# An expert's rows in parts: two halves of the down product in two banks, a write for each tile of rows

## What is computed

```python
w_topk, e_topk = jax.lax.top_k(probs, TOP_K)                 # 2 of 8 experts
buf = jnp.zeros((E, CAPACITY, H)).at[e_flat, pos].set(x_rep, mode='drop')
h = _rms(buf, norm_w[:, None, :])
gate = jax.nn.gelu(jnp.einsum('ech,ehf->ecf', h, Wg), approximate=False)
up = jnp.einsum('ech,ehf->ecf', h, Wu)
buf_out = jnp.einsum('ecf,efh->ech', gate * up, Wd) + buf
exp_out = buf_out[e_flat, jnp.minimum(pos, CAPACITY - 1)]
combined = x + (w_topk.reshape(-1)[:, None] * exp_out * keep).reshape(N, TOP_K, H).sum(axis=1)
```

## Time and profile before

| | |
|---|---|
| median of 3 runs | 454.93 us (454.25 to 458.86) |
| the profiled execution, own time | 458.62 us |
| its span, first to last instruction | 456.9 us |
| mean granted clock of TensorE, 1.00 being 2.4 GHz | 0.934 |
| busy share of the span: PE, DVE, POOL, ACT | 85%, 68%, 59%, 49% |
| chain that ended last, by engine | PE 60%, DVE 14%, issue 7%, POOL 6%, DMA 5% |

### The profile page before, as it was taken

How to read it: one execution, slowest core, us unless ns; L and a number is a source line. 1 busy time by engine, 2 the same in 40 slices (tenths; PEclk the granted TensorE clock), 3 DMA queues, 4 the chain that set the end, 5 groups by cost and what they waited for, 6 DMA issues and landing times.

```text
span 456.9 us, 7235 instructions
## 1 busy us (share of the span) xinstructions
PE 390.0 (85%) x2470; PEld 180.1 (39%) x2470; DVE 309.9 (68%) x722; ACT 223.6 (49%) x498; POOL 268.3 (59%) x242
## 2 busy tenths in 40 slices
PE   8985869999999999999899889998777697998810
PEld 2432524444334344444345334432324343654510
DVE  4786877757876867777966998864376456665514
ACT  1550433867776667667586655666630121322200
POOL 7383183678559688478586569688504350355650
PEclk9998998999999999999999999998985588999985
DMA  8594766005505009705005000008100011221118
GB/s 240 88 293 118 117 135 96 16 0 105 143 1 108 2 5 248 230 22 87 2 13 95 3 0 9 15 18 279 58 0 30 26 49 52 70 83 60 44 47 275
DMA packets 30461, 37.48 MB, mean 82 GB/s; under 512 B 4757, under 2 KB 25045, under 8 KB 30101
## 3 DMA queue, kind: packets, MB, share of 16 engines
q1 hardware_dynamic: 24378, 29.91, 27.6%
q0 software_dynamic: 2240, 4.21, 3.0%
q10 hardware_dynamic: 3808, 2.92, 2.3%
HBM read 28.56 MB, written 12.75 MB: 90 GB/s over the span
## 4 chain that ended last, share of the span: by engine, by line
PE 60%; DVE 14%; issue 7%; POOL 6%; DMA 5%; ACT 3%; SPq 2%; another core or an unknown queue 2%; POOLq 0%; DVEq 0%; ACTq 0%
PE ps_av L1128 14%; PE ps_st L1099 12%; PE ps_slot L1020 12%; DVE neg_max L1346 5%; PE ps_slot L1024 5%; POOL parts L800 3%; PE ps_st L964 3%; PE ps_slot L1159 2%; PE ps_st L1203 2%; DMA k_parts<-part_all 2%; ACT probs L910 1%; POOL probs L732 1%; PE ps_st L1107 1%; PE ps_slot L1213 1%
## 5 line engine op out<-in xcount | busy, mean ns | idle before, releaser
L910 ACT ACTIVATE probs<-ps_st 128x512 f32<-128x512 f32 (+3 forms) x384 | 168.5, 494 | 106.5 <-PE ps_st L1099 99.9
L1346 DVE TENSOR_REDUCE neg_max<-ps_slot 128x1 f32<-128x640 f32 (+7 forms) x184 | 175.8, 989 | 56.8 <-PE ps_slot L1024 54.7
L732 POOL TENSOR_TENSOR probs<-probs,f_all 128x960 f32<-128x960 f32 (+2 forms) x65 | 123.7, 1904 | 10.3 <-ACT probs L910 5.5
L1020 PE MATMUL ps_slot<-k_stack,q_stack 128*128 128x512 bf16 (+3 forms) x384 | 101.0, 333 | 10.5 <-DVE neg_max L1346 5.6
L1099 PE MATMUL ps_st<-q_stack,k_stack 128*128 128x512 bf16 (+3 forms) x384 | 104.0, 331 | 4.8 <-ACT probs L910 3.6
L1128 PE MATMUL ps_av<-probs,v_all 128*9 128x512 f32 (+3 forms) x768 | 81.1, 496 | 2.3 <-POOL probs L732 1.6
L729 POOL TENSOR_SCALAR_AFFINE_SELECT probs<-probs 128x512 f32<-128x512 f32 x58 | 37.1, 639 | 68.4 <-ACT probs L910 68.2
L1024 PE MATMUL ps_slot<-b_all,flip_b 128*128 128x240 bf16 (+2 forms) x288 | 66.5, 256 | 0.0
L1099 PEld LDWEIGHTS ps_st<-q_stack,k_stack 128*128 128x128 bf16 x384 | 34.6, 98 | 76.9 <-ACT probs L910 54.8
L1020 PEld LDWEIGHTS ps_slot<-k_stack,q_stack 128*128 128x128 bf16 x384 | 36.0, 99 | 44.5 <-DVE neg_max L1346 12.3
L800 POOL DMA_INDIRECT parts<-probs,e_tok x32 | 31.1, 972 | 38.1 <-DVE probs L1661 27.4
(11 more groups left out here) (188 smaller groups left out, 408.0 us busy)
## 6 DMA issues: line engine op xcount, KB each, us to landing
q_stack<-q_parts SPq DMA_DIRECT2D x21, 192.0 KB
slots<-in_c_rows_dram SPq DMA_DIRECT2D x4, 528.0 KB, 9.9
probs<-slots SPq DMA_DIRECT2D x8, 264.0 KB
parts<-in_c_rows_dram SPq DMA_DIRECT2D x4, 512.0 KB, 9.6
q_stack<-parts SPq DMA_DIRECT2D x4, 512.0 KB, 5.5
k_stack<-k_parts SPq DMA_DIRECT2D x14, 128.0 KB
f_all<-g_vec ACTq DMA_DIRECT2D x1, 1536.0 KB, 12.6
q_parts<-part_all SPq DMA_DIRECT2D x16, 96.0 KB, 3.5
```

The lines of the kernel that those rows point to most:

```text
L732: pool.tensor_tensor(pr, pr, f_of[:, n % (H // HG), :, fo:fo + hi - lo], ALU.mult).then_inc(near_done, 1)
L910: act.activation(probs[:, u % PBUF, g, c0:512], ps_st[:, ST_NO[what] % 3, c0:512], ACT.Exp, scale=SCALE).then_inc(exp_done, 1)
L1020: pe.matmul(ps_slot[:, slot, o + lo:o + hi], q_stack[:, buf, t // MT, g, t % MT * P:(t % MT + 1) * P], k_stack[:, buf, lo // CW, g, 0:hi - ...
L1346: dve.tensor_reduce(neg_max[:, t // MT, heads[0]:heads[-1] + 1, t % MT], src, AX.X, ALU.max, negate=True).then_inc(slot_used, 1)
```

## The change

The down product is split: the tiles of rows 0 and 1 go to `ps_slot[:, 0, ...]`, the bank that the transposes of the same buffer use, tiles 2 and 3 to `ps_slot[:, 1, ...]` as before. Each half raises `eo_ps`. Each scale waits for its own half. Each write waits for its own scale. The row numbers are made in `weights_of_rows`, in arrays with a place for every expert, and raise semaphores of their own (`row_done`, `tok_done`). Since transposes now share a bank with rows 0 and 1, `turn` waits until two tiles of the expert before in that buffer are scaled.

```diff
-        e_row_tok = sb("e_row_tok", [P, 2, 4])
-        e_tok = sb("e_tok", [P, 2, 4], U32)
+        e_row_tok = sb("e_row_tok", [P, E_NUM, 4])
+        e_tok = sb("e_tok", [P, E_NUM, 4], U32)
...
             def scatter_rows(e, i):
-                pool.wait_ge(eo_done, 6 * (e + 1))
+                pool.wait_ge(tok_done, e + 1)
                 for j in range(4):
+                    pool.wait_ge(eo_done, 4 * e + j + 1)
...
                 if positive(e - 1):
                     pe.wait_ge(eT_sb, e - 1)
+                    pe.wait_ge(eo_done, 4 * (e - 2) + 2)
...
-                        mm = pe.matmul(ps_slot[:, 1, i * 512 + j * C:i * 512 + (j + 1) * C],
+                        mm = pe.matmul(ps_slot[:, j // 2, i * 512 + j * C:i * 512 + (j + 1) * C],
...
-                mm.then_inc(eo_ps, 1)
+                    if j % 2:
+                        mm.then_inc(eo_ps, 1)
...
                 dve.tensor_tensor(e_wt[:, i, 2, :], e_wt[:, i, 0, :], e_wt[:, i, 1, :], ALU.mult).then_inc(ewt_done, 1)
+                dve.tensor_tensor(e_row_tok[:, e, :], e_row_tok[:, e, :], e_wt[:, i, 0, :], ALU.subtract).then_inc(row_done, 1)
                 dve.wait_ge(ewt_done, 2 * e + 1)
                 dve.tensor_tensor(e_wt[:, i, 2, :], e_wt[:, i, 2, :], a2, ALU.add).then_inc(ewt_done, 1)
+                dve.wait_ge(row_done, e + 1)
+                dve.tensor_copy(e_tok[:, e, :], e_row_tok[:, e, :]).then_inc(tok_done, 1)
...
             def scale_rows(e, i, n):
-                dve.wait_ge(eo_ps, e + 1)
                 if positive(n):
                     dve.wait_ge(scattered[i], 64 * n)
-                dve.tensor_tensor(e_row_tok[:, i, :], e_row_tok[:, i, :], e_wt[:, i, 0, :], ALU.subtract).then_inc(eo_done, 1)
-                dve.wait_ge(eo_done, 6 * e + 1)
-                dve.tensor_copy(e_tok[:, i, :], e_row_tok[:, i, :]).then_inc(eo_done, 1)
                 for j in range(4):
-                    dve.tensor_scalar(e_out[i][:, j, :], ps_slot[:, 1, i * 512 + j * C:i * 512 + (j + 1) * C], e_wt[:, i, 2, j:j + 1], None,
+                    dve.wait_ge(eo_ps, 2 * e + j // 2 + 1)
+                    dve.tensor_scalar(e_out[i][:, j, :], ps_slot[:, j // 2, i * 512 + j * C:i * 512 + (j + 1) * C], e_wt[:, i, 2, j:j + 1], None,
                                       ALU.mult).then_inc(eo_done, 1)
```

More of the change, by code:

```diff
@@ L472, in layer_kernel @@
         eo_done = sem("eo_done")
+        row_done = sem("row_done")
+        tok_done = sem("tok_done")
         scattered = [sem(f"scattered{i}") for i in range(2)]
@@ L797, in scatter_rows @@
             def scatter_rows(e, i):
-                pool.wait_ge(eo_done, 6 * (e + 1))
+                pool.wait_ge(tok_done, e + 1)
                 for j in range(4):
-                    pool.indirect_dma_start(parts[:, :], bass.IndirectOffsetOnAxis(ap=e_tok[:, i, j:j + 1], axis=0),
+                    pool.wait_ge(eo_done, 4 * e + j + 1)
+                    pool.indirect_dma_start(parts[:, :], bass.IndirectOffsetOnAxis(ap=e_tok[:, e, j:j + 1], axis=0),
                                             e_out[i][:, j, :], None, bounds_check=2 * (B * T + 2 * CAP) - 1,
@@ L1632, in weights_of_rows @@
                 if positive(e - 1):
-                    dve.wait_ge(eo_done, 6 * (e - 1))
+                    dve.wait_ge(eo_done, 4 * (e - 1))
                 a1, a2 = slot_in[i][:, :, C], slot_in[i][:, :, C + 1]
-                dve.tensor_scalar(e_row_tok[:, i, :], slot_in[i][:, :, C + 3], 2.0, 1.0, ALU.mult,
+                dve.tensor_scalar(e_row_tok[:, e, :], slot_in[i][:, :, C + 3], 2.0, 1.0, ALU.mult,
                                   ALU.add).then_inc(ewt, 1)
```

## The result

The changed kernel takes 454.23 us (median of 20 runs, 450.75 to 460.97) against 456.76 us for the kernel before on the same chip (median of 20 runs, 453.03 to 460.84): **a ratio of 0.9936, with a 95% interval of 0.9917 to 0.9955**. That is 2.0 to 3.8 us faster; the ratio leaves out slow runs, the medians do not. The forecast was 2.0 us slower. The measured time lies in the forecast's range, and the change is under the 1% that was given a chance of 0.70, but it went the other way.

What follows compares the result with a forecast made beforehand. It took TensorE to bound the expert stage up to about 420 us and GpSimd's row writes from 421. Waits of +3.6 and early writes of -1.6 gave +2.0 us on the median 454.93: 456.9 us, range 453.0 to 460.5.

Steps and rivals of the forecast that it cites:

- Regimes and GpSimd's price: Expert stage: TensorE's pace to about 420 us, 5.7 us an expert; GpSimd's row writes from 421 us, 5.1 an expert.
- Early writes, 1.6 us: GpSimd's writes for experts 6 and 7 start after the first scale, so the end comes 1.6 us earlier.
- The waits of single writes: Three writes an expert get their own wait on GpSimd: taken as nothing, upper bound 2.9 us at the end.
- Row numbers ahead and restart: Row numbers moved before VectorE's gating: 0.10 us an expert; TensorE restarting after each new wait: 0.15 us.
- The new wait, 3.6 us: TensorE's transposes wait for two scaled tiles: 2.44 us over experts 0 to 4, 3.6 later with restarts and row numbers.
- The two disturbances: Late scales of experts 2 and 4, releaser unnamed: TensorE idle 0.94 and 2.04 us, lower clock behind them about 1.7.
- three signs of being wrong: Transposes start without waiting, end writes over 1.3 us apart, or granted clock below 1.00 between 395 and 415 us.
- Rival 3: Both disturbances in the expert stage go, saving 4.7 us: 448.6 to 452.2 us, chance 0.08.
- rival 1: TensorE's new waits add up, the forecast itself: 455.7 to 459.5 us, centre 456.9, chance 0.55.
- Rivals 2 and 4: Waits hidden, only the gain left: 453.3 us, chance 0.17; disturbances become serial: 459.2 with one, 461.5 with two, chance 0.12.
- The clock (rival 5): TensorE's clock falls in the new waits, 1.7 us a fall: 458.6 with one, 460.3 with two, chance 0.08.
- The rule on the shared port: VectorE in two-port mode would hold GpSimd's writes up to 0.34 us, 2.7 at the end; the sum held nothing.

Runs made afterwards that it cites:

- late_writes: Changed kernel, but GpSimd waits for all four scales of an expert before writing its first tile: 457.18 us, ratio 0.9984.
- half_writes: Kernel before, but GpSimd writes only rows 0 and 1 of each expert, leaving out half the routed rows: 446.01 us, ratio 0.9813.
- landed: Kernel before, but GpSimd begins an expert's writes only when those of the expert ahead have landed: 457.36 us for one run (kernel before beside it 454.44).
- other_bank: Changed kernel, but rows 0 and 1 of the down product go where the other buffer's transposes were, so the wait is met at once: 453.81 us, ratio 0.9945.

## Why the prediction was wrong, step by step

- **Regimes and GpSimd's price.** The price was right: 969 to 992 ns a write, 1.28 apart at the end. The second regime was not the stage's own: GpSimd's hold on the chain from 421 us on began with the second disturbance, and without it GpSimd holds only the last four writes.
- **Early writes, 1.6 us.** Right: the last write stands 1.52 us nearer to expert 7's down product, and the first write of expert 1 starts 1.18 us after its first scale (1.1 forecast). Taken back by *late_writes*, the ratio goes from 0.9936 to 0.9984, about 2.2 us, with intervals that touch and late counts that came back with it, so this is no clean price; the trace shows 0.54 us in the way to the end. The waits of single writes cost nothing: 0.30 before expert 7's first write, the usual pause.
- **Row numbers ahead and restart.** The row numbers, 0.10 an expert, cost nothing that the rows show: from the first instruction of `weights_of_rows` to the gating it is 1.66 us with them (406.17 to 407.83) and was 1.67 at expert 4 without them (413.15 to 414.82). The restart was put at 0.15; a step grew by 0.95 us with 0.77 of idle time in it, which leaves 0.18.
- **The new wait, 3.6 us.** Right in kind, too small in size: 5.2 us. The forecast took the lateness from single experts of before (0.22 to 0.81) and had 4.4 for six experts at full clock; it left expert 5 out for a low clock that was the second disturbance's. In the settled rhythm each gating starts 1.38 us behind the down product (406.45 to 407.83 above), as late as at expert 4 before, where expert 1 had 1.15; that makes 0.77 each time. The difference comes for the most part from one instruction. The second half of the fold starts 0.50 us into a row write (406.82 and 407.32 above) and takes 0.59 us, in all five such experts, and as much in the changed kernel with the loads ahead, where no slot load runs; in *half_writes*, where no write stands beside it, it takes 0.33 to 0.35. At expert 1 and at expert 4 before:

```profile
396.10 0.33 DVE L1623 TENSOR_SCALAR probs<-k_stack,e_norm 128x256 f32<-128x256 f32 x1
...
414.31 0.59 DVE L1623 TENSOR_SCALAR probs<-k_stack,e_norm 128x256 f32<-128x256 f32 x1
```

- **The two disturbances: the step that failed.** The sum was made on an execution that had them, and held them to be the same after the change: "the terms come from the stage's own steps, not from the disturbances". They are a result of how GpSimd's writes follow one another, and the change alters that: they cost 5.2 us before, and after it no idle time of that kind is left. A term of -5.2 us that the sum held at 0 is what turned its sign. The forecast even had the pieces: it priced GpSimd's writes, and eight of them follow one another from 407.42 to 417.33 in the timeline of before, just ahead of the second disturbance. It did not ask what was under way when each count was late, and none of its three signs of being wrong looked at the disturbances: transposes waited, writes stood 1.28 us apart and the clock stayed at 1.00, as it said.
- **Rival 3 is what happened**, with rival 1's waits inside it, and had 0.08. The argument against it was that the median of the three runs shown, 454.93, lay 3.7 us below the profiled execution, "as if it lacked them already". Later medians of the kernel before were 454.44 to 457.70, and its second trace had both disturbances at a time of 457.39, the median of its runs being 457.08. A median of three runs could not carry that argument. From 456.76 rival 3's sum, + 2.0 - 4.7, gives 454.06; 454.23 was measured. That it fits so closely is luck: the waits came out 1.6 us larger than in that sum and the disturbances 0.5 larger, and the traces account for 1.5 us where the medians differ by 2.5. Nor was it a change of over 1%, as the forecast counted it: its plain sum of 452.2 lay 0.6% under 454.93.
- **Rivals 2 and 4.** No: the waits are not hidden (the chain runs through them), and the disturbances did not become serial, since they went.
- **The clock (rival 5).** It stayed at 1.00 through six waits of up to 0.83 us. The loop that the Trainium skill describes in "TensorE: Matmul & The Clock Gate", section "HAM oscillation — how this bites in real kernels", does not set in here; in the page's example the wait is longer than the work between two waits, here it is 0.77 us in 6.62. In the run with the wait alone two of four waits of some 2 us were followed by a fall.
- **The rule on the shared port.** The Trainium skill, "SBUF — State Buffer", section "SBUF: two separate sides", would have held writes beside scales, if a scale ran in a two-port mode. All 32 writes lie between 969 and 992 ns; the one that starts at 432.83 runs beside scales from 432.65 and 433.47 and takes 0.97 us. No run here shows a write that is held. What the rows show is the reverse, which the forecast had nothing for: VectorE's fold is 0.24 us longer beside a write (above).

**What was shown, and what was argued.** That the row writes hold the counts back is shown by *half_writes*; that a wait between groups of writes is enough to prevent it, by *landed*; that neither TensorE's wait nor its absence decides it, by *landed* and *late_writes*. Pauses of 1.8 us (changed kernel) and 2.1 us (*landed*) behind four writes were enough, pauses of 0.85 and 1.05 us (*other_bank*) were not. That the wait works in the changed kernel by making that pause is argued from its rhythm: four writes take 3 x 1.28 + 0.97 = 4.8 us and an expert 6.62, so 1.8 are left. Open are the path on which a write delays a count of TensorE, and what it is about the writes: the number in a row, their rate (four in 6.6 to 6.9 us did little harm, four in 5.7 did), or how many are still under way. Open too is a part of the size: the traces give 1.5 and 1.7 us from expert 0's down product on, the two ratios 2.0 to 3.8 and 1.3 to 3.3 us.

## What to carry to other kernels

An idle time whose releaser the profile cannot name is not noise until a second trace lacks it: look up what else runs at that moment on every engine and queue, and ask whether the change alters that. If an engine issues small indirect writes one behind the other while other engines hand work over by TensorE's counts, try a pause between groups of them, or fewer of them; the pause has its own price, and *landed* gained nothing by it. And a wait added on the busiest engine has two sides: it costs its own length at each turn, but it also spaces all that follows from it.

## What the hardware showed that was not expected

- Counts of TensorE reached ScalarE and VectorE up to 3.6 us after the recorded end of the matmul that carried them, with GpSimd's indirect writes of 128 rows under way 1.28 us apart; TensorE's own matmuls ran on meanwhile. With two writes an expert (pause 3.40 us), all steps but the last were 5.65 to 5.68 us.
- The price of eight experts with four writes each instead of two: 67.36 to 67.59 us against 59.59 from expert 0's down product to the end. Two writes fewer at the end account for 2 x 1.28 = 2.6 of these 7.8 to 8.0 us; the other 5.2 to 5.4 are the late counts and what follows from them.
- A fold of 128x256 f32 on VectorE that starts 0.50 us into one of these writes takes 0.59 us instead of 0.33 to 0.35, and ends 0.12 us behind the write; the writes themselves stay at 0.97 us.
